# Retrieval weights of a decoder kernel: products of side exponentials in place of exponentials of pair sums

## The reference, cut to what matters

```python
sim = jnp.einsum('pbthn,hkpn->pbthk', q, keys)
scores, idx = lax.top_k(sim, K_PER_HEAD)
sx, sy = (scores[0], scores[1])
all_scores = (sx[..., :, None] + sy[..., None, :]).reshape(b, t, N_HEADS, K_PER_HEAD * K_PER_HEAD)
sc, pk = lax.top_k(all_scores, K_PER_HEAD)
...
z = jnp.einsum('btd,bthkd->bthk', h, de)
z = act(z * jax.nn.softmax(sc, axis=-1))
out = jnp.einsum('bthk,bthkd->btd', z, ue)
```

## Time and profile before

| | |
|---|---|
| median of 3 runs | 1243.58 (1241.71 to 1244.4) |
| the profiled execution: time, span | 1244.53, 1242.5 |
| busy over the span | TensorE 925.8, VectorE 854.0, ScalarE 599.1, GpSimd 486.2 |
| L766 `mask`, 64 in three groups by buffer, the largest | 39 of mean 3350 ns |
| L775 `weigh` | 64 of mean 2314 ns |
| L703 exponential, L711 Silu | 1981 ns, 1881 ns |
| L631 pair sum, the largest group | 39 of mean 3646 ns |

### The profile page before, as it was taken

The page is one execution under the profiler, slowest core; times in us unless marked ns, Lnnn a source line. Parts: engine busy times, 40 slices in busy tenths (PEclk is TensorE's granted clock), DMA queues, the critical chain, the costliest instruction groups (busy, mean ns, idle before and its releaser), DMA issues. The chain is left out here.

```text
span 1242.5 us, 14693 instructions
## 1 busy us (share of the span) xinstructions
PE 925.8 (75%) x5514; PEld 651.1 (52%) x5537; DVE 854.0 (69%) x1200; ACT 599.1 (48%) x693; POOL 486.2 (39%) x298
## 2 busy tenths in 40 slices
PE   5669898239789797897997957695767777667990
PEld 2334744138678686786894336453233333445770
DVE  4774203999999999999821457584999999342442
ACT  2213031674877678667731033126988888312220
POOL 1124002864555655655201012301877776240005
PEclk9769989669899998998997988798677767678995
DMA  3010020000000000000002000390799889215113
GB/s 118 1 68 1 1 107 1 0 1 1 1 1 1 1 1 1 1 1 1 1 1 90 0 1 1 146 296 8 155 185 179 178 162 172 59 56 165 51 52 118
DMA packets 155448, 73.95 MB, mean 60 GB/s; under 512 B 138813, under 2 KB 151297, under 8 KB 154178
## 3 DMA queue, kind: packets, MB, share of 16 engines
q1 hardware_dynamic: 153842, 68.81, 22.2%
q0 software_dynamic: 1536, 4.20, 1.1%
HBM read 27.90 MB, written 11.53 MB: 32 GB/s over the span
## 5 line engine op out<-in xcount | busy, mean ns | idle before, releaser
L677 PE MATMUL r_head_sum<-ident,r_w 128*128 128x128 f32 (+1 forms) x2048 | 243.4, 283 | 45.2 <-DVE x L781 24.7
L677 PEld LDWEIGHTS r_head_sum<-ident,r_w 128*128 128x128 f32 (+1 forms) x2048 | 241.8, 199 | 51.4 <-issue 51.2
L631 POOL TENSOR_TENSOR r_pair_sum<-r_sims 128x2025 f32<-128x2025 f32 x39 | 142.1, 3646 | 148.6 <-DVE r_w L766 93.7
L1453 ACT ACTIVATE c_probs<-c_scores,c_bias,c_q_scale 128x1024 int16<-128x1024 f32 x128 | 154.2, 1205 | 34.6 <-DVE c_bias L1466 25.9
L1464 DVE TENSOR_REDUCE c_neg_max<-c_scores 128x1 f32<-128x1024 f32 x128 | 155.5, 1214 | 13.3 <-PE c_scores L1404 13.1
L775 DVE SCALAR_TENSOR_TENSOR r_w<-r_w,r_scale,r_z 128x2025 f32<-128x2025 f32 x64 | 148.0, 2314 | 10.7 <-PE r_z L645 10.5
L1391 POOL CAST c_rounded<-c_probs 128x1024 bf16<-128x1024 int16 x128 | 132.2, 1040 | 47.7 <-ACT c_probs L1453 46.4
L1404 PE MATMUL c_scores<-c_kT,c_placed 128*128 128x512 bf16 x233 | 100.2, 517 | 61.7 <-ACT c_probs L1453 53.2
L766 DVE SCALAR_TENSOR_TENSOR r_w<-r_pair_sum,r_kept,r_w 128x2025 f32<-128x2025 f32 x39 | 130.6, 3350 | 2.3 <-ACT r_w L703 2.2
L711 ACT ACTIVATE r_w<-r_w 128x2025 f32<-128x2025 f32 x64 | 116.1, 1881 | 4.3 <-DVE r_w L775 4.1
L703 ACT ACTIVATE r_w<-r_pair_sum,r_neg_max 128x2025 f32<-128x2025 f32 x39 | 77.0, 1981 | 37.8 <-PE r_head_sum L677 27.4
(11 more groups left out here) (277 smaller groups left out, 1596.0 us busy)
## 6 DMA issues: line engine op xcount, KB each, us to landing
ew_w<-in_w SPq DMA_DIRECT2D x2, 2992.0 KB, 15.4
sorted_rows<-ew_w SPq DMA_DIRECT2D x1, 4096.0 KB, 40.2
e_row<-sorted_rows SPq DMA_DIRECT2D x8, 512.0 KB, 7.2
expert_rows<-e_made SPq DMA_DIRECT2D x8, 512.0 KB, 3.2
ew_w<-in_w_near SPq DMA_DIRECT2D x1, 2176.0 KB, 25.8
ctxT<-in_ctxT SPq DMA_DIRECT2D x2, 1024.0 KB, 8.8
r_up<-in_up SPq DMA_DIRECT2D x1, 2048.0 KB, 10.0
c_pT<-c_rounded SPq DMA_TRANSPOSE x128, 2.8
```

The source lines that it names most:

```text
L631: nc.gpsimd.tensor_tensor(sums[u % SUMS].rearrange("p (a b) -> p a b", b=KEYS), a.broadcast_to([P, KEYS, KEYS]), b.broadcast_to([P, KEYS, ...
L677: last = nc.tensor.matmul(head_sum[0:m, b // 4, (b % 4) * P:(b % 4 + 1) * P], w[:, u % RING, b * P:b * P + m], ident[:, :], start=(h == 0 ...
L1453: nc.scalar.activation(probs[:, u % RING, :], scores[:, u % SCORED, :, :].rearrange("p a b -> p (a b)"), ACT.Exp, bias=bias[:, t, h:h + 1] ...
```

## The change

exp(a + b) is exp(a) times exp(b), so the exponential is taken of each side: 16 rows of 45 similarities and their 8 best, less the side's largest, 848 numbers for a tile in one instruction (`exps`). GpSimd now multiplies instead of adding, and only 36 of the 45 rows of a unit; ScalarE makes the other 9 as copies of 45 numbers, each scaled by a number read from `side_exp` (`last_rows`), three units ahead. VectorE's `choose` becomes `best_keys` (after unit 1) and `best_pairs` (before unit 0), the two passes become `pick` (at least the eighth best, times z) and `weigh` (pairs times that), and the softmax's scale goes into the Silu as its scale. Silu and row copies alternate from unit to unit; the side exponentials stand before unit 2. The residual moves from unit 6 to unit 3, the projection from unit 2 to unit 5 and waits for the picks alone, and the sums are copied in four parts, each with its own signal to `output`. GpSimd and the row copies wait until the buffer's unit, five back, is weighed. `w` has 9 rows instead of 10. In `attend` six semaphores do the work of twelve, and SP waits for transfer u - 6 before it issues u.

The diff, cut (removed functions stand in the kernel above):

```diff
-        RING = 10
...
+        RING = 9
+        SIDES = 2 * HEADS_R
+        WITH_BEST = KEYS + TOP
+        POOL_ROWS = 36
+        AHEAD = 3
+        CHOOSE_AT, EXP_AT, SUM_AT, ADD_AT, PROJECT_AT = 1, 2, 0, 3, 5
...
+        pairs = [pair_weight[:, k, :] for k in range(3)] + [a[:, :, :].rearrange("p c n -> p (c n)")[:, 0:PAIRS] for a in (sh.xT, sh.ctxT)]
+        MADE = len(pairs)
...
+        best = sb("best", [P, SIDES, TOP])
+        below_max = sb("below_max", [P, SIDES, WITH_BEST])
+        side_exp = sb("side_exp", [P, 2, SIDES, WITH_BEST])
...
-                    pool.wait_ge(sims_copied, t + 1)
-                if u >= SUMS:
-                    pool.wait_ge(masked, u - SUMS + 1)
...
+                    pool.wait_ge(exps_ready, t + 1)
+                if u >= MADE:
+                    pool.wait_ge(weighted, u - MADE + 1)
+                a = side_exp[:, t % 2, h, 0:POOL_ROWS].rearrange("p (a o) -> p a o", o=1)
+                b = side_exp[:, t % 2, HEADS_R + h, 0:KEYS].rearrange("p (o b) -> p o b", o=1)
+                nc.gpsimd.tensor_tensor(pairs[u % MADE][:, 0:POOL_ROWS * KEYS].rearrange("p (a b) -> p a b", b=KEYS),
+                                        a.broadcast_to([P, POOL_ROWS, KEYS]), b.broadcast_to([P, POOL_ROWS, KEYS]),
+                                        ALU.mult).then_inc(pairs_made, 1)
...
-                    pe.wait_ge(weighted, HEADS_R * t)
+                    pe.wait_ge(picked, HEADS_R * t)
...
-                pe.wait_ge(wT_copied, t + 1)
                 for b in range(PB):
+                    if b % 4 == 0:
+                        pe.wait_ge(wT_copied, 4 * t + b // 4 + 1)
...
-                if h == 2 and t + 1 < NT:
+                if h == PROJECT_AT and t + 1 < NT:
...
+            def exps(t):
+                act.wait_ge(below_ready, t + 1)
+                if t >= 2:
+                    act.wait_ge(weighted, HEADS_R * (t - 1))
+                nc.scalar.activation(side_exp[:, t % 2, :, :], below_max[:, :, :], ACT.Exp).then_inc(exps_ready, 1)
+
+            def last_rows(u):
+                t, h = divmod(u, HEADS_R)
+                if u >= MADE:
+                    act.wait_ge(weighted, u - MADE + 1)
+                for a in range(POOL_ROWS, KEYS):
+                    last = nc.scalar.activation(pairs[u % MADE][:, a * KEYS:(a + 1) * KEYS], side_exp[:, t % 2, HEADS_R + h, 0:KEYS],
+                                                ACT.Copy, scale=side_exp[:, t % 2, h, a:a + 1])
+                last.then_inc(rows_made, 1)
+
+            def silu(u):
+                t, h = divmod(u, HEADS_R)
+                act.wait_ge(weighted, u + 1)
+                nc.scalar.activation(w[:, u % RING, :], w[:, u % RING, :], ACT.Silu,
+                                     scale=scale[:, t % 2, h:h + 1]).then_inc(silu_done, 1)
+
+            def copy_sums(t):
                 act.wait_ge(summed, HEADS_R * (t + 1))
                 if t >= 1:
                     act.wait_ge(out_ready, t)
-                nc.scalar.copy(wT[:, 0:PB - 1, :].rearrange("p b n -> p (b n)"),
-                               head_sum[:, :, :].rearrange("p a b -> p (a b)")[:, 0:(PB - 1) * P])
-                nc.scalar.copy(wT[0:LAST, PB - 1, :], head_sum[0:LAST, 3, 3 * P:4 * P]).then_inc(wT_copied, 1)
+                for j in range(4):
+                    whole = min(4, PB - 1 - 4 * j)
+                    last = nc.scalar.copy(wT[:, 4 * j:4 * j + whole, :].rearrange("p b n -> p (b n)"), head_sum[:, j, 0:whole * P])
+                    if j == 3:
+                        last = nc.scalar.copy(wT[0:LAST, PB - 1, :], head_sum[0:LAST, 3, 3 * P:4 * P])
+                    last.then_inc(wT_copied, 1)
+
...
+            exps(0)
+            for u in range(AHEAD):
+                act.wait_ge(exps_ready, 1)
+                last_rows(u)
+            for t in range(2, NT):
+                copy_sims(t)
+            for u in range(UNITS):
+                t, h = divmod(u, HEADS_R)
+                if h == EXP_AT and t + 1 < NT:
+                    exps(t + 1)
+                if u + AHEAD < UNITS:
+                    last_rows(u + AHEAD)
+                silu(u)
+                if h == SUM_AT and t >= 1:
+                    copy_sums(t - 1)
+            copy_sums(NT - 1)
...
+            def best_keys(t):
...
+                for s in range(SIDES):
+                    last = nc.vector.max(best[:, s, :], sims[:, t, s, :])
                 chain.step(last)
-                a = best[:, 0, :, :].rearrange("p h (a o) -> p h a o", o=1).broadcast_to([P, HEADS_R, TOP, TOP])
-                b = best[:, 1, :, :].rearrange("p h (o b) -> p h o b", o=1).broadcast_to([P, HEADS_R, TOP, TOP])
-                chain.step(nc.vector.tensor_tensor(grid[:, :, :].rearrange("p h (a b) -> p h a b", b=TOP), a, b, ALU.add))
+                if t >= 1:
+                    dve.wait_ge(exps_ready, t)
+                top = best[:, :, 0:1]
+                nc.vector.tensor_tensor(below_max[:, :, KEYS:], best[:, :, :], top.broadcast_to([P, SIDES, TOP]), ALU.subtract)
+                nc.vector.tensor_tensor(below_max[:, :, 0:KEYS], sims[:, t, :, :], top.broadcast_to([P, SIDES, KEYS]),
+                                        ALU.subtract).then_inc(below_ready, 1)
+
+            def best_pairs(t):
+
+                dve.wait_ge(exps_ready, t + 1)
+                if t >= 2:
+                    dve.wait_ge(silu_done, HEADS_R * (t - 1))
+                a = side_exp[:, t % 2, 0:HEADS_R, KEYS:].rearrange("p h (a o) -> p h a o", o=1).broadcast_to([P, HEADS_R, TOP, TOP])
+                b = side_exp[:, t % 2, HEADS_R:, KEYS:].rearrange("p h (o b) -> p h o b", o=1).broadcast_to([P, HEADS_R, TOP, TOP])
+                chain.step(nc.vector.tensor_tensor(grid[:, :, :].rearrange("p h (a b) -> p h a b", b=TOP), a, b, ALU.mult))
...
+                chain.step(nc.vector.tensor_reduce(scale[:, t % 2, :], kept[:, t % 2, :, :], AX.X, ALU.add))
...
+            def pick(u):
                 t, h = divmod(u, HEADS_R)
                 if h == 0:
-                    scales(t)
                     dve.wait_ge(z_ready, t + 1)
-                dve.wait_ge(masked, u + 1)
-                nc.vector.scalar_tensor_tensor(w[:, u % RING, :], w[:, u % RING, :], scale[:, t % 2, h:h + 1],
+                dve.wait_ge(pairs_made, u + 1)
+                dve.wait_ge(rows_made, u + 1)
+                if u >= RING:
+                    dve.wait_ge(summed, u - RING + 1)
+                nc.vector.scalar_tensor_tensor(w[:, u % RING, :], pairs[u % MADE], kept[:, t % 2, h, TOP - 1:TOP],
                                                z[:, :, :].rearrange("p a b -> p (a b)")[:, 0:PAIRS],
-                                               ALU.mult, ALU.mult).then_inc(weighted, 1)
+                                               ALU.is_ge, ALU.mult).then_inc(picked, 1)
+
+            def weigh(u):
+                dve.wait_ge(picked, u + 1)
+                nc.vector.tensor_tensor(w[:, u % RING, :], pairs[u % MADE], w[:, u % RING, :], ALU.mult).then_inc(weighted, 1)
...
+            best_keys(0)
...
+                if h == 0:
+                    best_pairs(t)
+                pick(u)
                 if u >= 1:
                     weigh(u - 1)
-                if h == 1 and t + 1 < NT:
-                    choose(t + 1)
-                if h == 6 and t >= 1:
+                if h == CHOOSE_AT and t + 1 < NT:
+                    best_keys(t + 1)
+                if h == ADD_AT and t >= 1:
                     residual(t - 1)
             weigh(UNITS - 1)
             residual(NT - 1)
...
+        IN_FLIGHT = 6
-        turned = [sem("turned%d" % n) for n in range(TURNED)]
+        turned = [sem("turned%d" % n) for n in range(IN_FLIGHT)]
-            return 16 * (u // TURNED + 1)
+            return 16 * (u // IN_FLIGHT + 1)
+                if u >= IN_FLIGHT:
+                    sp.wait_ge(turned[u % IN_FLIGHT], turned_count(u - IN_FLIGHT))
-                sp.dma_start_transpose(pT[:, u % TURNED, :, :], rounded[:, u % ROUNDED, :]).then_inc(turned[u % TURNED], 16)
+                sp.dma_start_transpose(pT[:, u % TURNED, :, :], rounded[:, u % ROUNDED, :]).then_inc(turned[u % IN_FLIGHT], 16)
-                    pool.wait_ge(turned[(u - ROUNDED) % TURNED], turned_count(u - ROUNDED))
+                    pool.wait_ge(turned[(u - ROUNDED) % IN_FLIGHT], turned_count(u - ROUNDED))
-                pe.wait_ge(turned[u % TURNED], turned_count(u))
+                pe.wait_ge(turned[u % IN_FLIGHT], turned_count(u))
```

More of the change, by code:

```diff
@@ L473 @@
 UNITS = NT * HEADS_R
-BATCH = 4
 def retrieval_tables(nc, ctx, sh):
@@ L596, in weigh_experts @@
         sb, ps, sem = scope(nc, ctx, "r2_")
-        RING = 10
[L598 to L602, removed]
+        RING = 9
[4 more added lines that the diff above has]
+        CHOOSE_AT, EXP_AT, SUM_AT, ADD_AT, PROJECT_AT = 1, 2, 0, 3, 5
+        sims = sb("sims", [P, NT, SIDES, KEYS])
+        pair_weight = sb("pair_weight", [P, 3, PAIRS])
```

(38 more changed lines are left out.)

8 lines of the change are left out of this document (5 added, 3 removed).

## The result

The changed kernel takes 1199.53 us in the median of 4 runs (1189.07 to 1204.19), the one before 1243.62; the ratio is 0.9636, 95% interval 0.9572 to 0.970. The forecast was 1209.5, range 1192 to 1226. The measured time lies inside the range and 10 us under the forecast, outside the narrower 1203 to 1216 that the forecast gave itself.

| term | before | after | change | forecast |
|---|---|---|---|---|
| end of the second tile's first weigh | 286.99 | 273.00 | -14.0 | -8.6 |
| six periods | 6 x 51.23 | 6 x 47.76 | -20.8 | -7.4 |
| from there to the last residual | 68.54 | 47.40 | -21.1 | -18.1 |
| behind the last residual | 579.6 | 590.2 | +10.6 | 0 |

A forecast was written before the change was run, and what follows sets the result against it. VectorE was taken to bound the retrieval, with GpSimd setting its pace. Start -8.6, six periods -7.4 and end -18.1 sum to -34, so 1243.6 - 34.1 = 1209.5 us, range 1192 to 1226.

The forecast's parts named there:

- three signs of being wrong: VectorE idle in the steady part, ScalarE over 47 of 50 busy, or stages after the retrieval changing length.
- The unit: One head of one token tile in the retrieval: 5.22 us on VectorE, 0.71 less than before, with GpSimd's product at 2.94.
- Best pairs: Once a tile on VectorE: grid product held by GpSimd to 38.0, in all 4.6 us more than a plain unit.
- the stall of 1.49 is gone: VectorE's wait for z in the retrieval vanishes: TensorE delivers at 37.7 to 39.4, wanted at 40.2.
- The 3.2: Upper bound in us for ScalarE's nine row copies a unit, also the skill's figure without overlap, against 2.25 forecast.
- The end: Retrieval's last tile, first weigh to last residual: 49.6 to 51.3 us instead of 68.5, so -18.1.
- Cross attention: Six semaphores for twelve and SP's wait for transfer u - 6: no change in time.
- A: Retrieval: TensorE falls behind and z or the residual makes VectorE wait, 1.5 us a tile, 1222 us; chance 12%.
- B: Retrieval: the helpers on VectorE cost 1.5 us a tile more than forecast, about 1221 us; chance 10%.
- C: VectorE's product of two plain tensors isn't held by GpSimd, units of 4.48 us, 1162 us; chance 6%.
- D: ScalarE's pointer-scale copies need another table than Silu, two loads of 1.28 us in every unit, 1272 us; chance 4%.
- E: GpSimd's product is slower than the sum or gains nothing from fewer rows (3.65 us stays), 1266 us; chance 3%.

The follow-up runs named there:

- rows45: Changed kernel with GpSimd making all 45 rows of a unit and ScalarE none; 1216.80 us.
- grid_late: Changed kernel with two small unused maxima put in front of the grid product of the best pairs, so that it starts later; 1204.46 us.
- project4: Changed kernel with TensorE projecting z for the next tile before unit 4 instead of unit 5; 1183.52 us, ratio 0.9513.
- late_last: Changed kernel with only the residual of tile 6 moved behind unit 6 of the last tile instead of unit 3; 1217.04 us.
- cross_only: Kernel before the change with only the new cross attention (`attend`) edit; 1243.29 us, ratio 0.9993.
- between_gap: Changed kernel with projection before unit 4, 33 GpSimd rows, the 10.2 us pause, and best keys between pick and weigh; 1192.16 us.
- after: The changed kernel itself, without further edit; 1199.53 us, ratio 0.9636 to the kernel before.
- gap: Changed kernel with a 10.2 us pause (GpSimd filling six rows of w with zeros) between retrieval and block attention; 1195.81 us.

## Why the prediction was right, point by point

The rule that carried the forecast, that GpSimd holds VectorE, is shown. But the nearness of the total is in part luck, one step failed and one term was missing. Of the prediction's three signs of being wrong two came true: VectorE waits in the steady part, and the stages behind changed length. The third did not: ScalarE is busy 37 us of each 47.8.

- The unit: forecast 0.14 + 2.94 + 2.14 = 5.22, measured 5.12 (GpSimd 2.92, pitch 397.62 to 402.74). The picks and weighs were held and free as foretold; rows45 shows the cause.
- Best pairs: this step failed. I let the grid product be held to 38.0; it begins first and isn't. From the end of the sixth weigh to its own end it takes 0.6, not 3.6. Of these 3.0 the wait for z takes back 1.5; the other 1.5 are most of the 2.2 us by which the forecast period was too long, and the rest are units that are 0.1 shorter. grid_late shows it. At the start the same product begins 0.05 before GpSimd and takes 0.69, and the first weigh ends at 223.87, 3.5 sooner than the 227.4 of the forecast.
- z: "the stall of 1.49 is gone" was wrong, as a consequence. VectorE wants z at 36.6 behind the first weigh, 3.6 sooner than the 40.2 that I took, and TensorE delivers at 38.1, as computed (37.7 to 39.4). project4 shows that the lateness is worth 1.4 us a tile.
- ScalarE: 2.10 for the copies, forecast 2.25; hidden, as forecast. The 3.2 that the prediction sets beside it is nine of its dear copies of 0.36 end to end; the copies overlap.
- The end: -21.1 for -18.1; late_last shows its cause. TensorE had stood still for 1.00 only before its last tile, so the tile took 28.78 without the 1.9 for the slow clock that I had added, and the output took 7.18, not up to 8.86. The wait for the copy fell to 0.68, as forecast; in the steady part it is 1.60, because a Silu stands before the copy in ScalarE's list.
- Cross attention: nothing, as forecast; cross_only shows it.
- Behind the retrieval: forecast as unchanged, measured +10.6. The term was missing. It offset half of what the retrieval gained beyond the forecast: -55.9 instead of -34. Without it the total would have been about 1189, below the whole range of 1192 to 1226. That it was inside is luck.
- The rivals: A came true in its mechanism, as z makes VectorE wait 1.5 a tile, but not in its total, because the grid product was cheaper by more. B is refuted, as the helpers were cheaper and not dearer; C by the held weighs, 2.96; D by the copies, which have no table load among them; E by the product of 2.91 in the profile and by rows45.

That the loss is the clock's is shown: in all 14 profiles the rest is 590 or more where the block attention has at least three neighbouring stretches of 10 us at 0.50 to 0.52 between 640 and 710, below 580 where it has at most one in a row, and the same 16 matmuls take 14.02 there and 7.39 otherwise.

What brings the stretch about is open. It isn't the retrieval's work alone: one and the same kernel has runs of both kinds (between_gap 1177.19 and 1193.15, after 1189.07 and 1204.19, as far as their mean clocks tell), and pauses of 5.2 and 10.2 worked in opposite ways on the same retrieval. The profiles show a difference of timing. When the matmuls with `b_conv_w` begin, the first of the block attention's own, the clock is at 0.50 in 13 of the 14. In the seven with the loss it rises to 1.00 some 3 to 4 us after their start and falls again 24 us later, although TensorE has been busy nearly all the time (in after 22.5 of 23.5). In six of the seven without it rises 5.5 to 6.3 us after their start, in gap just before it, and stays at 1.00 for 47 to 52 us. So the moment at which these matmuls begin, seen from the clock's rise, goes with the loss in every profile. That it is the cause is not shown: no run moved that moment by a few us in small steps.

## What to carry to other kernels

Before costing a VectorE instruction with two SBUF operands, ask whether it or GpSimd's begins first: 0.15 us ahead the grid product took 0.68, 0.31 us behind it took 3.19. Where one engine lags and finishes alone, moving its start forward is worth as much as the work saved in the loop. Compare stages, not totals: a gain of 56 us in one stage came with a loss of 11 in another that nobody touched.

## What the runs showed of the hardware

VectorE's instruction with two SBUF operands and GpSimd's product don't run side by side here. Begun second, VectorE's stood still until GpSimd's was over (3.19 for 0.68, the weighs 2.96 for 2.26); begun first, it ran freely and GpSimd's took 3.34 for 2.91. Picks, with one operand in PSUM, took 2.31 throughout.

TensorE's granted clock stayed at 0.50 for 51 us (644 to 695), in the first 30 of which TensorE was busy without a gap, and directly before it had been at 1.00 for 24 us with TensorE busy nearly throughout. The Trainium skill, "TensorE: Matmul & The Clock Gate", section "What's actually happening", has activity release the throttle; this stretch doesn't agree. A pause of 10.2 us removed the stretch in the changed kernel and not in the one with 33 rows, where one of 5.2 us removed it.
